# Moving the experts' weight loads from ScalarE's queue to SyncE's in a fused scan, attention and mixture-of-experts kernel

## What is computed

```python
x = x + L0(_gn(x))                  # state-space layer, see below
t = _to_tokens(x)
t = t + L1_attn(_ln_t(t))           # linear attention, 8 heads of 16
t = t + L1_ffn(_ln_t(t))            # 8 experts, the best 2 of each token
```

```python
logits = x @ Wg; top_logits, top_idx = top_k(logits, 2); top_w = softmax(top_logits)
h = x @ W1[e]; g = x @ W3[e] + b3[e]
out = sum over the two chosen e of top_w * ((silu(h) * g) @ W2[e])     # 128 -> 384 -> 128
```

## Time and profile before

| what | value |
|---|---|
| median of 3 runs | 4227.19 us (4223.45 to 4231.14) |
| profiled execution | 4220.52 us, its span 4218.1 us |
| PE, PEld busy | 3292.7 us (78%), 1992.9 us (47%) |
| DVE, ACT, POOL busy | 3006.8 us (71%), 2556.1 us (61%), 2917.0 us (69%) |
| queue 1 (SP's transfers) | 484.12 MB, 46.4% of the 16 DMA engines' span |
| queue 10 (ACT's transfers, the weights alone) | 203.47 MB, 16.1% |
| transfers by ACT | w_up 344, w_down 344 |
| transfers by SP | dt_rep 384, x_stack 576, u_in 344, rows_out 344, dt_dram 192, others some 350 |

### The profile page before, as it was taken

How to read it: one execution, slowest core, us unless ns; L and a number is a source line. 1 busy time by engine, 2 the same in 40 slices (tenths; PEclk the granted TensorE clock), 3 DMA queues, 4 the chain that set the end, 5 groups by cost and what they waited for, 6 DMA issues and landing times. The chain is left out here.

```text
span 4218.1 us, 69032 instructions
## 1 busy us (share of the span) xinstructions
PE 3292.7 (78%) x17432; PEld 1992.9 (47%) x17432; DVE 3006.8 (71%) x5234; ACT 2556.1 (61%) x6173; POOL 2917.0 (69%) x3055
## 2 busy tenths in 40 slices
PE   5687887888788868887788877889778977777473
PEld 2233343344465535653455534555356543557462
DVE  3699998888867977778766877678776788732210
ACT  3465765476567656675566765677556764767352
POOL 1466675867576876779577785768767696857665
PEclk9798997898799978998899987999789998999796
DMA  4865655555677657965678556785668755967584
GB/s 103 194 164 130 150 138 123 142 135 149 174 208 214 156 148 187 240 170 147 161 206 219 146 152 176 210 214 141 163 170 229 195 144 149 250 186 226 152 244 118
DMA packets 420321, 730.04 MB, mean 173 GB/s; under 512 B 56201, under 2 KB 313810, under 8 KB 417746
## 3 DMA queue, kind: packets, MB, share of 16 engines
q1 hardware_dynamic: 302418, 484.12, 46.4%
q10 hardware_dynamic: 99072, 203.47, 16.1%
q0 software_dynamic: 18432, 37.93, 3.3%
HBM read 596.93 MB, written 100.07 MB: 165 GB/s over the span
## 5 line engine op out<-in xcount | busy, mean ns | idle before, releaser
L638 POOL TENSOR_TENSOR prod<-state,c_rep 128x384 f32<-128x384 f32 x1536 | 1530.2, 1002 | 899.3 <-DVE state L1471 867.5
L1471 DVE TENSOR_TENSOR_SCAN state<-dt_rep,carry,ps_x 128x384 f32<-128x384 f32 x1280 | 1284.4, 1003 | 6.5 <-issue 5.1
L1458 DVE TENSOR_TENSOR ps_x<-ps_x,db_rep 128x384 f32<-128x384 f32 x1536 | 854.3, 556 | 457.9 <-PE ps_x L824 417.1
L1097 ACT ACTIVATE dt_rep<-dt_rep,vecs 128x384 f32<-128x384 f32 x1536 | 916.7, 612 | 170.1 <-DMA dt_rep<-dt_dram 91.0
L824 PE MATMUL ps_x<-x_stack,copy 96*128 96x384 bf16 x1536 | 546.6, 357 | 350.1 <-DVE state L1471 344.1
L810 PE MATMUL ps_conv<-gx,w_conv 128*128 128x384 f32 x1728 | 703.9, 528 | 9.2 <-DVE parts L1488 6.0
L824 PEld LDWEIGHTS ps_x<-x_stack,copy 96*128 96x128 bf16 x1536 | 155.8, 102 | 850.3 <-DVE state L1471 606.6
L977 PE MATMUL ps_h<-u_t,w_up 128*128 128x128 f32 x2064 | 330.0, 299 | 220.1 <-DVE silu L1681 206.9
L1285 ACT ACTIVATE g_sb<-ps_g,w_down 128x128 f32<-128x128 f32 x1032 | 303.4, 368 | 211.5 <-PE ps_g L996 178.0
L810 PEld LDWEIGHTS ps_conv<-gx,w_conv 128*128 128x128 f32 x1728 | 321.7, 203 | 226.7 <-issue 120.2
L977 PEld LDWEIGHTS ps_h<-u_t,w_up 128*128 128x128 f32 x2064 | 280.1, 203 | 309.7 <-issue 194.5
(11 more groups left out here) (235 smaller groups left out, 4987.2 us busy)
## 6 DMA issues: line engine op xcount, KB each, us to landing
dt_rep<-dt_dram SPq DMA_DIRECT2D x384, 768.0 KB
w_up<-in_w_exp ACTq DMA_DIRECT2D x344, 384.0 KB
w_down<-in_w_exp ACTq DMA_DIRECT2D x344, 193.5 KB
x_stack<-parts SPq DMA_DIRECT2D x576, 48.0 KB
u_in<-rows_in SPq DMA_DIRECT2D x344, 64.5 KB
rows_out<-u_out SPq DMA_DIRECT2D x344, 64.0 KB
dt_dram<-dt SPq DMA_DIRECT2D x192, 96.0 KB
qv<-in_x SPq DMA_DIRECT2D x48, 192.0 KB
```

Of the source, the lines that this page charges most:

```text
L638: pool.tensor_tensor(prod[:, k % HS, :], state[:, k % HS, :], c_rep[:, c % 2, :], ALU.mult).then_inc(s_prod.sem, 1)
L1097: act.activation(dt_rep[:, g % XS, q, :], dt_rep[:, g % XS, q, :], ACT.Exp, scale=decay_rate).then_inc(s_decay.sem, 1)
L1458: dve.tensor_tensor(x_n, x_n, db_rep[:, c % 2, :], ALU.mult).then_inc(s_inflow.sem, 1)
L1471: dve.tensor_tensor_scan(state[:, k % HS, :], dt_rep[:, g % XS, q, :], ps_x[k % XB][:, 0:T], init, ALU.mult, ALU.add).then_inc(s_state.sem, 1)
```

## The change

The function `weights` goes from ACT's program to SP's. There it waits itself: for the sorting before tile 0, and for ACT's reading of bank g of tile u-3 before tile u. It is called at t = 303, 305, 307 for the first three tiles and at t = TILE[u-3] + 3 for the others, ahead of the loads of u_in and the stores of u_out of the same step. `apart()` raises a semaphore and waits for nothing. ACT keeps its own wait for s_down before L1285. The buffers, the sizes and the number of the transfers stay.

```diff
--- before.py
+++ after.py
@@ -558,9 +558,24 @@
                     due(sp, s_acc, m, NC)
                     sp.dma_start(image_rows(acc_dram, m), acc.rearrange("p k d -> p (k d)")).then_inc(s_accout.sem, 16)
 
+            def weights(m, u):
+                if u == 0:
+                    due(sp, s_sorted, m, 2)
+                    apart()
+                if u >= WA:
+                    sp.wait_ge(*read(m, f"g{u - WA}"))
+                    apart()
+                e = sp.value_load(expert_of[0:1, parity(m), u:u + 1], min_val=0, max_val=NE - 1)
+                tall = a["w_exp"][bass.ds(e, 1)].rearrange("o p f -> p (o f)")
+                sp.dma_start(w_up[:, u % WA, :], tall[:, 0:2 * F]).then_inc(s_up[u % WA].sem, 16)
+                sp.dma_start(w_down[:, u % WB, :], tall[:, 2 * F:3 * F + MF]).then_inc(s_down[u % WB].sem, 16)
+
             def experts(m, t):
                 if m is None:
                     return
+                for u in range(NU):
+                    if t == (T_W + 2 * u if u < WA else TILE[u - WA] + 3):
+                        weights(m, u)
                 for u in range(NU):
                     if t == (T_LOAD + u if u < 2 else max(T_LOAD + u, TILE[u - 2] - 4)):
                         if u == 0:
@@ -1259,12 +1274,6 @@
                         act.wait_ge(*full(m, "ctx" if kind == "qT" else "ao5"))
                     evacuate(m, name, turned[:, T * g:T * g + T], o)
 
-            def weights(m, u):
-                e = act.value_load(expert_of[0:1, parity(m), u:u + 1], min_val=0, max_val=NE - 1)
-                tall = a["w_exp"][bass.ds(e, 1)].rearrange("o p f -> p (o f)")
-                act.dma_start(w_up[:, u % WA, :], tall[:, 0:2 * F]).then_inc(s_up[u % WA].sem, 16)
-                act.dma_start(w_down[:, u % WB, :], tall[:, 2 * F:3 * F + MF]).then_inc(s_down[u % WB].sem, 16)
-
             def tile_up(m, u):
                 if u < NU:
                     tanhs()
@@ -1290,8 +1299,6 @@
                         due(act, s_ostore[v % UOUT], m, v // UOUT)
                     ins = act.activation(u_out[:, v % UOUT, :], aux(name)[:, F:F + P], ACT.Copy, scale=u_in[:, v % UIN, D:D + 1])
                 ins.then_inc(frees(name), 1)
-                if u + WA < NU:
-                    weights(m, u + WA)
 
             def attention(m, t):
                 if m is None:
@@ -1339,12 +1346,6 @@
             def experts(m, t):
                 if m is None:
                     return
-                for u in range(WA):
-                    if t == T_W + 2 * u:
-                        if u == 0:
-                            due(act, s_sorted, m, 2)
-                            act.sem_inc(s_sp.sem, 1)
-                        weights(m, u)
                 for u in range(2):
                     if t == T_TILE - 2 + u:
                         evacuate(m, f"T{u}", u_t[:, u % UT, :], aux(f"T{u}")[:, 0:P])
```

## The result

| | before | after |
|---|---|---|
| median of 20 runs each, one chip | 4231.34 us | 4206.19 us |
| profiled execution, its span | 4220.52, 4218.1 us | 4205.15, 4202.2 us |
| transfers on SP's queue 1 | 484.12 MB | 687.59 MB |
| transfers on ACT's queue 10 | 203.47 MB | none |

The ratio of the two means is 0.9948, with a 95% interval of 0.9934 to 0.9961: 22 us faster at 4227 us, so about 4205 us, where 4216 us were forecast (11 us faster). The medians alone are 25 us apart. The medians of one chip are compared with each other, since the same kernel before had 4220 to 4231 us as its median on the chips of this study.

The account below looks back on a forecast made before the run. No engine is full; hand-overs between engines bound the kernel, PE and POOL nearest to full. Gains of 17 and 4 less losses of 9 and 1 make 11 us: 4227.2 - 11 = 4216 us, range 4184 to 4246 us.

Parts of the forecast that it names:

- the loop at the end: Image 7's tiles: weights issued later on SP make a three-tile loop of 9.4 us, 3.15 us a tile, 9 us lost.
- the gain in passes 2 to 6: Passes with a scan: freeing ACT's queue gains its 1.1% of the chain over 1515 us, 17 us.
- the loss at the start of image 7: Before image 7, the second and third weights calls delay u_in 2: 1 us lost, between 0 and 3.
- The upper bound, 66.8 us: Passes with a scan: ACT's idle time before L1097 ended by its own issuing, the most that could be gained.
- rival A: ACT as hidden pace-maker: 35 us gained in passes, 10 us in image 6, nothing lost in image 7; 4182 us, chance 0.13.
- Image 6: Image 6's tiles in the last pass: a quarter of 15 us of chain, 4 us gained, ends 0 and 15.
- SP's added time costs nothing in the passes: Passes with a scan: 1.5 us a call on SP is covered by its existing waits and the dt_rep lead; cost nothing.
- a landing of 4.0 us: Image 7's loop: assumed time for w_up from issue to use, between bounds of 3.2 and 5.5 us.
- rival B: Image 7's tiles: w_up lands in 5.5 us, so the loop costs 31 us; 4242 us, chance 0.20.
- The register load: In each weights call: 278 ns from the trace; the skill's 600 ns floor would make the whole sum 6 us gained.
- Rival D: Passes with a scan: w_up queued behind dt_rep makes PE wait, 39 us in all; 4255 us, chance 0.06.
- the row before L1097: Sign of right: ACT's idle time there that ended with issuing falls from 66.8 us to under 25 us.

Follow-up runs that it names:

- e12: The changed kernel run again unaltered, on another chip; ratio to the kernel before 0.9964 (0.9941 to 0.9987).
- the five: The changed kernel and four follow-up runs with its code in the passes; mean 2410.1 us for passes 2 to 6, 155.1 us for image 6's tiles.
- e11: The changed kernel with two further register loads in each weights call on SP; ratio to the kernel before 1.017.
- e1: The changed kernel with SP waiting for PE's filling of bank g, not ACT's reading, one step earlier; ratio to the kernel before 0.9964.
- e7: The kernel before the change with two further register loads in each weights call on ACT; ratio to the kernel before 1.0181.

## Why the prediction was right, step by step

The direction, the places of gain and loss and the loop at the end were right; the size of the gain was half of what this pair of kernels showed (22 us) and three quarters of what the second chip showed (15 us, e12). Two terms were too small, the gain in passes 2 to 6 by 11 us and the loss at the start of image 7 by 2.5 us; their signs are opposite and pass 7 gave 2 us back, so that the sum by stages (17 us) lies nearer to the forecast than its largest term does.

**The mechanism in the passes was right, its size too small.** Forecast: 17 us over six images, from 1.1% of the chain between 3570 and 3700 us. Measured: some 28 us in passes 2 to 6, and 2 us back in pass 7. Two things were wrong with the term. The chain was read in one stretch of 130 us, late in the run, and carried over to 1515 us of passes; its eleven pieces all belong to three calls between 3591 and 3603 us. And a share of the chain is what the instructions hold themselves; that their removal also brings the engines behind ACT closer fits DVE's waits for ACT (62 to 45 us), but how much each of the two made isn't shown. The upper bound, 66.8 us, was no better: 64 us of that row went, and 28 us came of it, since 60 us came back as ACT's waits for PE. Passes were to come about 3 us closer and came 5.5 us closer (28 by 5), which was the mark set for rival A. A, with 35 us for the passes, was as near as the forecast there and wrong in taking image 7's loss as nothing.

**Image 6**: forecast 4 us gained, measured 4.9 us in the pair of profiles and 4.1 us as the mean of the five. The quarter of the chain's 15 us was a guess that held; the wait for w_up that took its place (8.3% of the chain) is the likely reason why it was no more, which no run sets apart. The forecast had no such wait in this stage.

**SP's added time costs nothing in the passes**: right as far as it goes, ACT's wait for dt_rep went from 7.2 to 7.5 us. e11 gives the margin that the forecast didn't: 1.1 us more a call costs about 20 us in the passes and 21 us with image 6.

**Image 7's loop** was right nearly to the digit: 3.15 us forecast, 3.15 us measured over tiles 3 to 42, 8.9 us lost there against 9. Its terms were a delay of 1.5 us (1.74 measured), a landing of 4.0 us, and 3.9 us (3.8 measured, as the median). Of the landing two rows with PE waiting are shown above: from the issue at 4039.95 to PE's start at 4043.64, 3.7 us, and from 4042.60 to 4047.21, 4.6 us, either with the hand-over to PE in it; the median of the 26 is 3.9 us. The rival B, a landing of 5.5 us, is out. But 4.0 us had been chosen between two bounds, 3.2 and 5.5 us, and at 5.5 us the loop would have cost 31 us: that it came out so near is in part luck. Why both waiting tiles of the kernel before had 5.5 us isn't shown. And the 1.5 us of delay assumed that SP stands waiting when L1300 ends, which it did at fewer than half of the tiles. What the forecast missed beside it is SP's own queue: 1.1 us a tile before (worked out above from its waits) and 1.5 us for the call make 2.6 us, measured 2.8, under a tile of 3.15 us. These two numbers could have been added up from the trace of before; they tell that a cure of the delay can give at most some 0.3 us a tile; e1 gave 0.17.

**The start of image 7** was undersized: 1 us, with 3 as its bound, against 3.5 us. The place was the right one (u_in of tile 2 behind weights), but only the calls were counted. acc_in stands ahead of it as well and waits for the landing of the store of out (3.6 us from 3991.40), which now is itself issued behind a call.

**The register load** was taken at the trace's 278 ns against the Trainium skill's floor of about 600 ns (DMA: Bandwidth & Descriptors, Latency and other measured facts). SP's 272 ns bears the trace out on the second engine too. What one more load adds to a call is another number, 0.54 us in e7 and 0.56 us in e11, since register instructions follow each; the forecast had them in its 0.7 us. Rival D, by which order in one queue makes w_up wait behind dt_rep, gave 39 us in the passes: PE waited 3.6 us and PEld 9.6 us there for w_up, so its sign is present and small; whether a dt_rep stood ahead of those transfers isn't shown.

**The signs that it had named.** Four of the five for right came: the row before L1097 fell to 2.7 us, SP's wait moved in part, PE waits for w_up at 26 of image 7's tiles, and the period is 3.15 us. The fifth, images about 3 us closer, did not; they came 5.5 us closer, which stood among the signs of wrong.

The sum is then, by stages: passes 2 to 6 about 28 gained, pass 7 2 lost, image 6 4 gained, image 7 12.4 lost, some 17 us; 11 were forecast, and the two measured ratios give 22 and 15 us.

## What to carry to other kernels

When issuing work moves to another engine's queue, add up that queue's own time for a tile (the stretch less its waits) and set it against the tile of each stage, the densest above all: the change took SP from 2.7 to 4.0 of some 6 us in the passes, from 0.9 to 2.6 of 3.7 us in image 6, and from 1.1 to 2.8 of 3.15 us at the end. Follow the moved transfer's loop there too, from the event that frees the buffer to the use. And where two stages want different owners, let each have its own: with ACT issuing for the last image alone, that image's steady tiles had their old length and the passes kept their gain.

## What was not expected of the hardware

Nothing in one instruction: load and issue cost the same on SP and ACT (272 and 278 ns, 348 and 349 ns). What was not expected is how steeply a queue's time turns into the kernel's: 0.6 us less in ACT's call gave 16 us, 1.1 us more cost 76 us; 1.1 us more in SP's call cost 87 us. Of the 370 to 390 us added to a queue in each of the last two, a fifth came out at the end.
